# A 16-image fusion model on one Trainium2 core: rounding of spikes put into the third norm, expert sums read by flat rows of 512, token lists built from quarter lanes

## The reference, cut to what matters

```python
h = concatenate([patches @ w + b, txt], axis=1)
h = h + gated_attention(layernorm(h))          # layer 0: kernel = relu(rope(q k))**2
h = h + expert_choice_ffn(layernorm(h))        # 32 experts, each takes its top 274 tokens
h = h + spiking_attention(layernorm(h))        # layer 1
h = h + routed_ffn(layernorm(h))               # shared + 2 of 8 experts

# expert_choice_ffn
G, idx = top_k(softmax(x @ W_router).T, 274)   # per expert
y = zeros.at[idx].add(G * (silu(x[idx] @ W_up) @ W_down))

# spiking_attention
spike = lambda x: floor(clip(x, 0, 4) + 0.5)
qkv = spike(x) @ Wqkv.T
qkv = (qkv - mean) * rsqrt(var + 1e-5)         # over all 8768 tokens, then q, k, v = spike(...)
```

## Time and profile before

| what | before |
|---|---|
| median of 3 runs (lowest, highest) | 1818.33 us (1817.97, 1819.61) |
| the profiled execution: its time, its span | 1819.5 us, 1817.9 us |
| TensorE busy, mean granted clock | 1400.6 us (77%), 0.895 |
| Vector engine busy | 1157.1 us (64%) |
| ScalarE, GpSimd busy | 676.9 us (37%), 789.1 us (43%) |
| DMA | 60.61 MB in 68912 packets |

### The profile page before, as it was taken

How to read it: one execution, slowest core, us unless ns; L and a number is a source line. 1 busy time by engine, 2 the same in 40 slices (tenths; PEclk the granted TensorE clock), 3 DMA queues, 4 the chain that set the end, 5 groups by cost and what they waited for, 6 DMA issues and landing times. The chain is left out here.

```text
span 1817.9 us, 27840 instructions
## 1 busy us (share of the span) xinstructions
PE 1400.6 (77%) x9079; PEld 998.9 (55%) x9079; DVE 1157.1 (64%) x1859; ACT 676.9 (37%) x1146; POOL 789.1 (43%) x827
## 2 busy tenths in 40 slices
PE   5679999999854313867728646888898789999998
PEld 3557777777533302756615432333334478788787
DVE  2755555555367781211114787888885798889898
ACT  3134444444434211322203346788775511111111
POOL 1444444444320034888754008777752333233331
PEclk9889999999975566998857888999999899999999
DMA  4070000000001122444452000000001000000000
GB/s 164 1 283 1 0 0 0 0 0 0 1 0 25 35 66 68 93 86 79 72 139 71 5 2 1 2 0 0 0 1 40 0 10 13 13 9 13 13 13 17
DMA packets 68912, 60.61 MB, mean 33 GB/s; under 512 B 15680, under 2 KB 63054, under 8 KB 67550
## 3 DMA queue, kind: packets, MB, share of 16 engines
q1 hardware_dynamic: 53073, 48.56, 8.3%
q0 software_dynamic: 13760, 10.23, 4.3%
q10 hardware_dynamic: 2016, 1.00, 0.2%
HBM read 35.36 MB, written 25.00 MB: 33 GB/s over the span
## 5 line engine op out<-in xcount | busy, mean ns | idle before, releaser
L1819 PE MATMUL at_slot<-at_qm,at_ks 128*128 128x512 bf16 (+1 forms) x640 | 160.4, 384 | 19.9 <-DVE at_clip L2024 9.9
L501 PE MATMUL ga_kv<-ga_kern,ga_v 128*128 128x274 f32 x512 | 133.5, 403 | 13.5 <-ACT ga_kern L590 12.5
L2540 DVE TENSOR_REDUCE mx_routed<-mx_weighted 128x128 f32<-128x1024 f32 x69 | 138.0, 2000 | 2.4
L2498 POOL TENSOR_TENSOR mx_h_E<-mx_hid_E,mx_h_E 128x768 fp32r<-128x768 f32 x23 | 43.6, 1895 | 188.9 <-DVE mx_h_E L2530 188.9
L83 PE MATMUL mx_e<-ff_expert_out_high,mx_h_E 128*128 128x512 f32 x276 | 111.4, 404 | 12.3 <-DVE mx_weighted L2537 12.3
L1903 ACT ACTIVATE at_clip<-at_slot,at_four 128x1024 bf16<-128x1024 f32 (+1 forms) x96 | 106.8, 1112 | 32.6 <-PE at_slot L1819 30.8
L2024 DVE TENSOR_SCALAR at_clip<-at_slot 128x1024 bf16<-128x1024 f32 (+1 forms) x96 | 116.2, 1218 | 3.4 <-PE at_slot L1819 3.0
L1421 POOL DMA_INDIRECT moe_sums<-ex_y,slot_sums x69 | 108.3, 1570 | 22.7 <-issue 22.1
L501 PEld LDWEIGHTS ga_kv<-ga_kern,ga_v 128*128 128x128 f32 x512 | 92.2, 189 | 37.8 <-ACT ga_kern L590 16.7
L84 PE MATMUL mx_e<-ff_expert_out_low,mx_h_E 128*128 128x512 f32 x276 | 108.7, 394 | 0.0
L85 PE MATMUL mx_e<-ff_expert_out_high,mx_h_E 128*128 128x512 f32 x276 | 108.6, 393 | 0.0
(11 more groups left out here) (447 smaller groups left out, 3856.7 us busy)
## 6 DMA issues: line engine op xcount, KB each, us to landing
moe_sums<-ga_zeros SPq DMA_DIRECT2D x8, 1152.0 KB, 16.5
ar_rows<-moe_sums SPq DMA_DIRECT2D x32, 256.0 KB
ex_down<-in_down SPq DMA_DIRECT2D x32, 192.0 KB, 2.5
token_rows<-ct_rows SPq DMA_DIRECT2D x17, 256.0 KB, 2.4
out_h<-H SPq DMA_DIRECT2D x22, 192.0 KB, 1.9
H<-in_text SPq DMA_DIRECT2D x1, 4096.0 KB, 21.4
patches<-in_patches SPq DMA_DIRECT2D x1, 1728.0 KB, 8.0
ga_sin<-in_sin SPq DMA_DIRECT2D x1, 1644.0 KB, 9.0
```

Of the source, the lines that this page charges most:

```text
L501: last = nc.tensor.matmul(kv[:, e, 0:HALF], v[p][:, mt + 2 * side, e * P:(e + 1) * P], kern[(p + g) % 2][:, side, :], start=mt == 0 and si ...
L1819: last = nc.tensor.matmul(to[r0:r0 + r, g % 2, :].rearrange("p (s n) -> p s n", s=2), ks[m][:, t * P:t * P + r], qm[m][:, 2 * g:2 * g + 2, ...
L2540: nc.vector.tensor_reduce(R[p][t][:], weighted[:].rearrange("p e d -> p d e"), AX.X, ALU.add).then_inc(reduced, 1)
```

## The change

1. `gated_attention`: the cut of W1 and `tokens_low` come first on the Vector engine; the eight zeroings follow, and the memset of `zeros` comes behind the first q and k parts.
2. `choose_tokens`: CUTS = 4, so a cut is one batch of 548 tokens, a round has four of each pass and four indirect DMAs, and there are 32 planes. The lists are read by two DMAs, of 64 and of 5 rows, and summed by five adds that fold the planes in halves.
3. `add_rows`: 17 groups of 512 rows and a tail of 64, regardless of batches. Partition p holds 4 rows in a run of 2 KB. Two DMAs a group, loops written out.
4. A new block `spike_norm` in place of `layernorm` "ln3". Its TensorE and ScalarE parts are those of `layernorm`, and W is loaded and cut at its start. The product also takes the maximum with 0. GpSimd does the step with UPWARD and MAGIC (`lift`), and the Vector engine subtracts MAGIC and takes the minimum with 4 (`land`) to a bf16 tensor `spikes` of all tokens, three products behind.
5. `project_qkv` has no rounding any more; TensorE reads `spikes` at an address worked out in the loop.

```diff
-CUTS = 2
+CUTS = 4
+EVEN_TILES = TILES // 16 * 16
...
+            nc.vector.tensor_copy(W1p[0][:], W1[:]).then_inc(w_cut, 1)
+            dve.wait_ge(w_cut, 1)
+            nc.vector.tensor_tensor(W1p[1][:], W1[:], W1p[0][:], ALU.subtract).then_inc(w_cut, 1)
+            tokens_low(0, 0)
             for p in range(2):
                 for parts in (hs_tail[p], key_tail[p]):
                     for part in parts:
                         nc.vector.tensor_scalar(part[:, :, tail:GAP], halves(k["ident"][:, 0:2 * (GAP - tail)]), 0.0, None, ALU.mult)
-            nc.vector.memset(zeros[:], 0.0).then_inc(zeros_set, 1)
-            nc.vector.tensor_copy(W1p[0][:], W1[:]).then_inc(w_cut, 1)
-            dve.wait_ge(w_cut, 1)
-            nc.vector.tensor_tensor(W1p[1][:], W1[:], W1p[0][:], ALU.subtract).then_inc(w_cut, 1)
-            tokens_low(0, 0)
             low_of(0, 0, 0)
             low_of(0, 0, 1)
+            nc.vector.memset(zeros[:], 0.0).then_inc(zeros_set, 1)
...
-            dve.wait_ge(lists_in, 16)
-            nc.vector.tensor_reduce(lst[:], lst_i[:].rearrange("t l x -> t x l"), AX.X, ALU.add).then_inc(lists_f, 1)
+            dve.wait_ge(lists_in, 32)
+            n, folds = PLANES // 2, 1
+            nc.vector.tensor_tensor(lst[:, 0:n], lst_i[:, 0:n], lst_i[:, n:2 * n], ALU.add).then_inc(lists_f, 1)
+            while n > 1:
+                dve.wait_ge(lists_f, folds)
+                n, folds = n // 2, folds + 1
+                nc.vector.tensor_tensor(lst[:, 0:n], lst[:, 0:n], lst[:, n:2 * n], ALU.add).then_inc(lists_f, 1)
...
-            sp.dma_start(lst_i[:], slots_d.rearrange("(l t i) j -> t l (i j)", l=PLANES, t=TILES)).then_inc(lists_in, 16)
+            by_tile = slots_d.rearrange("(l t i) j -> t l (i j)", l=PLANES, t=TILES)
+            for t0, t1 in ((0, EVEN_TILES), (EVEN_TILES, TILES)):
+                sp.dma_start(lst_i[t0:t1], by_tile[t0:t1]).then_inc(lists_in, 16)
...
+        NBUF, J = 4, 4
+        WIDTH = J * P
+            for g, (at, r, j) in enumerate(groups):
+                p = g % NBUF
+                if g >= NBUF:
+                    sp.wait_ge(turned, g - NBUF + 1)
+                for q in range(2):
+                    sp.dma_start(rows[p][q][0:r, 0:j, :], y_d[q][at:at + r * j, :].rearrange("(p j) d -> p j d", j=j)).then_inc(loaded[p], 16)
...
+                nc.gpsimd.tensor_tensor(rows[p][0][0:r, 0:j], rows[p][0][0:r, 0:j], rows[p][1][0:r, 0:j], ALU.add).then_inc(joined, 1)
...
+                hb = H[:, at:at + r * j].rearrange("d (p j) -> d p j", j=j)
+                nc.vector.tensor_tensor(hb, hb, out_ps[p][:, 0:r * j].rearrange("d (j p) -> d p j", j=j), ALU.add).then_inc(summed, 1)
...
+def spike_norm(nc, k, x, H, XN, spikes, w3):
+    sets, nv, tag, LAG = NGRP, 1, "ln3", 3
...
+            def lift(i, g):
+                pool.wait_ge(scaled, scaled0 + 4 * i + g + 1)
+                nc.gpsimd.tensor_scalar(whole(XN, i, g), whole(XN, i, g), UPWARD, MAGIC, ALU.mult, ALU.add).then_inc(lifted, 1)
+
+            square(0, 0)
+            square(0, 2)
+            for t in range(sets + 1):
+                for g in (0, 2):
+                    if t + 1 < sets:
+                        square(t + 1, g)
+                    if t >= 1:
+                        lift(t - 1, g)
+                        lift(t - 1, g + 1)
...
+                nc.vector.scalar_tensor_tensor(dst, dst, 0.0, bc_ps[m % 2][:, :, 0:HALF], ALU.max, ALU.mult).then_inc(scaled, 1)
+
+            def land(n):
+                i, g = divmod(n, NGRP)
+                dve.wait_ge(lifted, n + 1)
+                nc.vector.tensor_scalar(whole(spikes, i, g), whole(XN, i, g), MAGIC, 4.0, ALU.subtract, ALU.min)
...
+            invert(0)
+            for t in range(1, sets + 1):
+                if t < sets:
+                    invert(t)
+                for g in range(NGRP):
+                    n = NGRP * (t - 1) + g
+                    scale(t - 1, g)
+                    if n >= LAG:
+                        land(n - LAG)
+            for n in range(B - LAG, B):
+                land(n)
...
                             for part in range(3):
                                 last = nc.tensor.matmul(q_ps[(3 * m + t) % NQ][:, j, 0:HALF], w3[:, part, t * P:(t + 1) * P],
-                                                        spikes[m % 2][:, j * HALF:(j + 1) * HALF], start=part == 0, stop=part == 2)
+                                                        spikes[:, bass.ds((NQ * i + m) * S + j * HALF, HALF)], start=part == 0, stop=part == 2)
```

More of the change, by code:

```diff
@@ L1545, in _ @@
         @block.gpsimd
         def _(pool):
-            with pool.Fori(0, B // NBUF) as i:
-                for p in range(NBUF):
-                    pool.wait_ge(loaded[p], 64 * i + 64)
-                    for n, t in ((P, slice(0, 4)), (tail, slice(4, 5))):
-                        last = nc.gpsimd.tensor_tensor(rows[p][0][0:n, t], rows[p][0][0:n, t], rows[p][1][0:n, t], ALU.add)
-                    last.then_inc(joined, 1)
+            for g, (at, r, j) in enumerate(groups):
+                p = g % NBUF
+                pool.wait_ge(loaded[p], 32 * (g // NBUF) + 32)
+                nc.gpsimd.tensor_tensor(rows[p][0][0:r, 0:j], rows[p][0][0:r, 0:j], rows[p][1][0:r, 0:j], ALU.add).then_inc(joined, 1)
@@ L1554, in _ @@
         @block.tensor
         def _(pe):
-            pe.sem_inc(summed, NBUF)
-            with pe.Fori(0, B // NBUF) as i:
-                for p in range(NBUF):
-                    c = NBUF * i + p
-                    pe.wait_ge(joined, c + 1)
-                    pe.wait_ge(summed, c + 1)
-                    for t in range(4):
-                        nc.tensor.transpose(out_ps[p][:, 0, t * P:(t + 1) * P], rows[p][0][:, t, :], k["ident"][:])
-                    nc.tensor.transpose(out_ps[p][:, 1, 0:tail], rows[p][0][0:tail, 4, :], k["ident"][0:tail, 0:tail]).then_inc(turned, 1)
+            for g, (at, r, j) in enumerate(groups):
+                p = g % NBUF
+                pe.wait_ge(joined, g + 1)
+                if g >= NBUF:
+                    pe.wait_ge(summed, g - NBUF + 1)
+                for t in range(j):
+                    last = nc.tensor.transpose(out_ps[p][:, t * r:(t + 1) * r], rows[p][0][0:r, t, :], k["ident"][0:r, 0:r])
+                last.then_inc(turned, 1)
@@ L1566, in _ @@
         @block.vector
         def _(dve):
-            with dve.Fori(0, B // NBUF) as i:
-                for p in range(NBUF):
-                    c = NBUF * i + p
-                    dve.wait_ge(turned, NBUF + c + 1)
-                    for at, n, bank in ((0, 4 * P, 0), (4 * P, tail, 1)):
-                        hb = H[:, bass.ds(c * S + at, n)]
-                        last = nc.vector.tensor_tensor(hb, hb, out_ps[p][:, bank, 0:n], ALU.add)
-                    last.then_inc(summed, 1)
+            for g, (at, r, j) in enumerate(groups):
+                p = g % NBUF
+                dve.wait_ge(turned, g + 1)
+                hb = H[:, at:at + r * j].rearrange("d (p j) -> d p j", j=j)
+                nc.vector.tensor_tensor(hb, hb, out_ps[p][:, 0:r * j].rearrange("d (j p) -> d p j", j=j), ALU.add).then_inc(summed, 1)
@@ L1693, in _ @@
[L1693 to L1702 removed]
+            nc.vector.memset(eps[:], 1e-5)
+            with dve.Fori(0, B // NQ) as i:
+                for m in range(NQ):
+                    c = NQ * i + m
+                    for t in range(3):
+                        n = 3 * c + t
+                        dve.wait_ge(kept, NQ + n + 1)
+                        dve.sem_inc(met, 1)
+                        for j in range(2):
+                            last = nc.vector.bn_stats(stats[:, t, bass.ds(2 * c + j, 1), :].rearrange("p a b -> p (a b)"),
+                                                      QKV[:, t, bass.ds(c * S + j * HALF, HALF)])
+                        last.then_inc(counted, 1)
@@ L2640, in build @@
         k["ln2_sems"] = {n: ctx.enter_context(nc.semaphore(f"ln2_{n}")) for n in LN2_SEMS}
+        k["ln3_sems"] = [ctx.enter_context(nc.semaphore(f"ln3_{n}")) for n in ("w_in", "cut", "lifted")]
         k["ln_sems"] = {n: [ctx.enter_context(nc.semaphore(f"ln_{n}")), 0] for n in LN_TOTALS}
```

226 lines of the change are left out of this document (143 added, 83 removed).

## The result

The changed kernel takes 1777.12 us (median of 4 runs, 1774.58 to 1780.33) against 1818.51 before: a ratio of 0.9773, 95% interval 0.9755 to 0.9791. The forecast was 1775, within 1764 to 1788.

A forecast was written before the change was run, and what follows sets the result against it. Stages run one after another, bounded mainly by the Vector engine in choosing and projection and by SP's DMA issue in add_rows. Savings 3.5 + 10.6 + 9.0 + 20.8 = 43.9 us from 1819.5 give 1775.6, some 1775 median; range 1764 to 1788.

The forecast's parts named there:

- Start of the attention: Gated attention: cut of W1 and tokens_low first let TensorE start near 96.8 instead of 100.36; -3.5 us, bounds -2 to -4.
- Rounds: Choosing tokens: quarters need 5 rounds of 7.4 us, set by GpSimd, instead of 8 of 6.26; -7.3 us with the front.
- The list's load: Choosing tokens: the list read in two parts takes 7.0 us instead of 11.8; -4.8 us, bounds 6.4 and 11.
- add_rows: The add_rows stage: 17 groups of 512 flat rows at 1.7 us each; -9.0 us, bounds -13.8 and -1.
- a buffer's turn: add_rows: with four buffers, a buffer's turn of 6.3 us sets 1.6 us a group, taken as 1.7 for queueing.
- the rival in which the loads hold it at 2.2 us: add_rows: loads stay the bound at 2.2 us a group, total 1783 us; chance 0.10.
- Norm: Third norm with rounding inside, W cut early: norm ends near 1017.0, TensorE starts at 1017.5 instead of 1020.33.
- The collision: Third norm, rival: lifts and lands share an interface and slow each other, sets of 9.0 us, total 1783; chance 0.14.
- Projection: Projection without rounding: groups at 0.74 us, end at 1058.3 against 1079.06; -20.8 us including TensorE's earlier start.
- the bound "hidden": Projection: TensorE's register step for each matmul is hidden, so a group stays at 0.70 us; 0.74 was taken.
- the rival of the register steps: Projection: unhidden register steps make a group 0.92 us; +8 us, total 1783; chance 0.08.

The follow-up runs named there:

- e11: Changed kernel with the eight zeroings and the memset of zeros ahead of W1's cut again, the old order; ratio 0.9795 to the kernel before.
- e8: Changed kernel with two sets of ids, five list rounds written out, waiting only for landings of the round before the last; ratio 0.974 to the kernel before.
- e3: Changed kernel with the list read by one DMA over all 69 rows; load 21.1 us, choosing 88.9 us against 85.0 before.
- e2: Changed kernel with two cuts of a lane instead of four; 1786.61 us, ratio 0.9811 to the kernel before.
- e7: Changed kernel with eight buffers in add_rows instead of four; ratio 0.9742 to the kernel before.
- e5: Changed kernel unchanged, run again for comparison; 1777.95 us, ratio 0.9775 to the kernel before.
- e9: Changed kernel with ten unread products on TensorE behind the norm's last broadcast; ratio 0.976 to the kernel before.
- e4: Changed kernel with add_rows of the kernel before, 16 batches of four DMAs; ratio 0.9818 to the kernel before.
- e1: Changed kernel with the third norm and projection of the kernel before; ratio 0.9933 to the kernel before.
- e6: Changed kernel with W loaded and cut ahead of the projection again, rounding still in the norm; ratio 0.9807 to the kernel before.

## Why the prediction was right, step by step

**Start of the attention** (-3.5): the product starts at 97.16, forecast 96.8. The zeroings and the memset did fit behind it, but for 0.1 us by the traces of before and after, or 0.5 by e11.

**Rounds** (-7.3 with their front): right in count and mechanism. 7.42 us a round were forecast as 7.4, set by GpSimd's four issues and the landing; e8 takes the wait away and the round falls to the Vector engine's 6.3. The second round, 8.3 us, was not foreseen. Loop and front measured -6.8.

**The list's load** (-4.8, measured -1.5): the term that was mis-sized. Its terms, 0.35 + 2.4 + 4.6, also add up to 7.35 us and not to 7.0 (and to 7.65 with its own 4.0 and 0.9 us for parts on 16 and 5 engines); the rest of the miss, 3.0 us, is mainly the price of a run. The number of engines for 69 rows was right (e3). The price was not: 29 ns came from the rate of add_rows divided by its share, a share that counted start, end and waits of that stage as if the rate would rise in proportion. With all 16 engines at work the load moves 175 to 210 GB/s, so 39 to 47 ns a run, and with the last rows issued last it is 10.4 us. It lies within the bounds given, 6.4 and 11. What follows for the change: e2 shows that quarters gain only some 0.4 us over halves in the stage. Most of what choosing gained (6.8 us) comes from the split read: by e2, halves with that read and the adds have 78.6 us against 85.0 before, 5.6 less in the load and 0.9 in the sums.

**add_rows** (-9.0): -8.6. The bound named first, a buffer's turn, is the right one (e7), and the rival in which the loads hold it at 2.2 us is wrong.

**Norm** (-2.8 to TensorE's start): -4.1 in the first trace, -3.0 in e5. The collision is there, at a third of the rival's price and in one set of two: a lift is 0.13 us longer, one land 0.9, a set 8.1 instead of 7.78. It is so in every trace of the new norm (7.8 and 8.1). The rival's sets of 9.0 us did not come. The Trainium skill ("GPSIMD Engine Reference", key points) names such contention for a two-port mode and for two SBUF inputs; that it falls on a land, which has one input, beside GpSimd's square, is what the row at 981.48 shows. Against add_rows the end came 1.6 us earlier than forecast: 0.7 had been allowed for collisions at the end and was not needed, and from the last set's first product to the last land it took 9.8 us instead of 10.3, as the eight pairs of product and land took 1.0 to 1.2 us each and hid most lifts.

**Projection** (-18.0 from TensorE's start on): -21.3 in the first trace, -20.2 in e5. Groups are 0.705 us, as the bound "hidden" has it, not 0.74, and the rival of the register steps falls. But not because they are hidden, as far as is shown: the prediction counted one for each matmul, and the trace has 32 of them for 288 matmuls.

```profile
L1798 PEldq FUSED_REGOPS  x32: 46/46/57, 997.4 to 1030.0; - x32
```

At 46 ns they would be 0.03 us a group even in the open. The groups at 0.705 instead of 0.74 are 1.5 us of what the projection took less than forecast; fewer groups at the slower clock are most of the rest.

**The median** is 2.1 above the forecast while the profiled execution, 1775.86, is 0.3 above its own of 1775.6: the profiled execution was one of the quicker two of four. (1775.6 less 1.2 is 1774.4, which the forecast rounded up to 1775.) e5's span, 2.6 us longer, has more than that in the norm, the projection and the attention, with the clock.

## What to carry to other kernels

A share of DMA time is no speed: a rate divided by a share below 1 says what the engines would do only if nothing but their idling were missing, so for a load of 512 B runs take the rate of a stretch in which they were all at work. When an edit doubles a list to shorten the loop that makes it, cost both ends: here they nearly cancel, and the split of the read, one line, is the gain. And where a stage is bound by a buffer's turn, a larger number of buffers is the cheapest test of it: here it was worth 4.4 to 4.9 us. A trace of the same stage in other runs tells what difference is still noise: e9's gain of 1.1 us is not beyond it, the 2.7 us in its projection are.

## What the runs showed of the hardware

**Short drops of TensorE's clock go with whole-kernel times that differ by several us.** In e2's attention, TensorE was busy for 0.37 of the 1.5 us from 1172.0, and was then granted half the clock for some 3.5 us. Two such drops in e2 go with an attention 5.3 us longer than that of e3 and e4, which have none, two in e1 with 3.4, and one each in e5, e6 and e11 with 275.9 to 276.5 us; without one it took 274.3 to 275.5:

```profile
1170.50:1172.00 1.50, 1.50 (x20) 0.75 (x20) 1.26 (x3) 1.40 (x4) 1.50 (x3) 1.00 0.00 0
1172.00:1173.50 1.50, 0.37 (x6) 0.30 (x5) 1.50 (x2) 1.02 (x2) 1.50 (x3) 0.94 0.00 0
1173.50:1175.00 1.50, 1.50 (x9) 0.75 (x9) 0.30 (x1) 0.72 (x1) 1.41 (x3) 0.50 0.00 0
1175.00:1176.50 1.50, 1.50 (x13) 0.46 (x12) 0.52 (x2) 0.14 (x1) 1.50 (x1) 0.50 0.00 0
```

What brings a drop about stays open: in e2 TensorE also paused for 1.1 us at 1281.5 and kept the full clock, and ahead of e5's drop, at 1325.2, it had no pause above 0.7 us.

**The experts took 231.4 to 231.8 us in all four kernels of e1 to e4 and 226.1 to 226.4 in the others after the change.** The granted clock in their second twelfth was 0.66 or 0.67 there and 1.00 in the first trace of the changed kernel, for the same code. What sets it was not tried.

**After a pause of TensorE the slow start of the projection lasted 2.8 us behind a pause of 9.7 (e6), 3.7 behind 8.9 (e1), and 3.4 to 5.7 behind 3.5 to 3.9 in the nine traces with an unchanged norm and projection**, so its length does not follow the pause's; filling the pause to about 1 us removed it, in both kernels in which it was tried.
